# Order of the second sequence's norm, queries and folds in a fused two-layer kernel

## The reference, cut to what matters

```python
x = x + xattn0(layernorm(x), ctx, ctx, ..., key_mask)   # 8 heads of 4
x = x + ffn0(layernorm(x), ...)                         # below
x = x + xattn1(layernorm(x), ctx, mask, ...)            # 16 heads of 64
x = x + ffn1(layernorm(x), ...)                         # small inner nets

def ffn0(x):            # C = 128, 16 heads of 8, 4 experts
    h = conv3(layernorm(x, ln1_w, ln1_b))               # depthwise, causal
    q, k, v = split(h @ attn_w); q, k = rope(q), rope(k)
    p = softmax(causal(q @ k.T / sqrt(8)))
    x = x + (p @ v) @ proj_w
    h = layernorm(x, ln2_w, ln2_b)
    e = argmax(h @ router_w)
    return x + expert[e](h)
```

## Time and profile before

| | us |
|---|---|
| three runs | 340.04, 342.58, 346.72 (median 342.58) |
| profiled execution, its time | 340.81 |
| its span, first to last instruction | 338.6 |
| PE / DVE / ACT / POOL busy | 315.3 / 245.2 / 220.0 / 128.1 |
| mean granted clock of PE | 0.993 |

### The profile page before, as it was taken

The page is one execution under the profiler, slowest core; times in us unless marked ns, Lnnn a source line. Parts: engine busy times, 40 slices in busy tenths (PEclk is TensorE's granted clock), DMA queues, the critical chain, the costliest instruction groups (busy, mean ns, idle before and its releaser), DMA issues.

```text
span 338.6 us, 6802 instructions
## 1 busy us (share of the span) xinstructions
PE 315.3 (93%) x2270; PEld 220.6 (65%) x2270; DVE 245.2 (72%) x758; ACT 220.0 (65%) x649; POOL 128.1 (38%) x183
## 2 busy tenths in 40 slices
PE   8799989998989999999989998998999999999886
PEld 3348778665554433345446998985778687878675
DVE  4988875784898988888811552479788877887576
ACT  1488885375365756756676765754676667686995
POOL 3455564110641444410640440410685434535400
PEclk9999999999999999999998999999999999999999
DMA  7590000076763430091001003100100000000002
GB/s 213 196 274 10 2 0 2 8 243 170 209 206 89 113 102 3 1 326 52 5 31 56 2 31 111 33 1 2 54 20 15 0 2 1 3 0 0 2 0 65
DMA packets 21881, 22.47 MB, mean 66 GB/s; under 512 B 3894, under 2 KB 18646, under 8 KB 21846
## 3 DMA queue, kind: packets, MB, share of 16 engines
q1 hardware_dynamic: 18982, 16.78, 17.4%
q10 hardware_dynamic: 2352, 4.20, 3.7%
q0 software_dynamic: 512, 1.05, 1.0%
HBM read 14.22 MB, written 7.60 MB: 64 GB/s over the span
## 4 chain that ended last, share of the span: by engine, by line
PE 58%; DVE 16%; ACT 14%; issue 5%; POOL 4%; DMA 3%; SPq 0%; ACTq 0%; POOLq 0%
PE PS L1388 51%; PE PS L1442 5%; DVE PS L872 5%; ACT big L1167 5%; ACT big L1364 3%; POOL big L529 2%; DVE big L690 2%; DVE big L715 2%; DMA big<-in_A_WkT 2%; ACT big L1305 1%; ACT big L1141 1%; DMA XN<-scr_y,pos 1%; DVE XN L667 1%; ACT cw L1141 1%; PE PS L1704 1%
## 5 line engine op out<-in xcount | busy, mean ns | idle before, releaser
L1388 PE MATMUL PS<-big 128*128 128x128 f32 (+10 forms) x592 | 93.3, 308 | 7.0 <-DVE big L690 2.1
L1388 PEld LDWEIGHTS PS<-big 128*128 128x128 f32 (+3 forms) x592 | 56.2, 150 | 39.7 <-DVE mB L872 18.2
L529 POOL TENSOR_TENSOR big<-big,urec 128x1024 f32<-128x1024 f32 x24 | 45.6, 1900 | 60.2 <-DVE urec L722 45.4
L1167 ACT ACTIVATE big<-big 128x154 f32<-128x154 f32 x192 | 60.5, 319 | 10.6 <-DVE big L690 5.6
L872 DVE CUSTOM_DVE_ANT_0 PS<-PS,later 128x128 f32<-128x128 f32 (+3 forms) x128 | 60.1, 517 | 8.9 <-PE PS L1388 7.7
L1305 ACT ACTIVATE big<-PS 128x1024 f32<-128x1024 f32 (+3 forms) x64 | 43.2, 701 | 25.0 <-PE PS L1388 25.0
L1141 ACT ACTIVATE big<-PS 128x1280 f32<-128x1280 f32 (+2 forms) x30 | 32.3, 1088 | 27.0 <-PE PS L1442 24.5
L1388 PE MATMUL PS<-kkC,XT 128*128 128x462 f32 (+1 forms) x96 | 36.0, 511 | 1.9 <-DVE big L715 1.9
L1167 ACT ACTIVATION_READ_ACCUMULATOR big<-big 128x1 f32 x192 | 36.2, 189 | 0.0
L517 POOL TENSOR_TENSOR rstd<-ve,minus_half 128x4 f32<-128x4 f32 (+2 forms) x13 | 13.2, 1017 | 56.3 <-DVE ve L662 56.3
L1388 PEld LDWEIGHTS PS<-vwCm,big 128*128 128x128 f32 x256 | 30.8, 192 | 3.9 <-ACT big L1141 1.3
(11 more groups left out here) (192 smaller groups left out, 499.7 us busy)
## 6 DMA issues: line engine op xcount, KB each, us to landing
scr_qk<-big SPq DMA_DIRECT2D x12, 384.0 KB, 3.3
big<-scr_qk SPq DMA_DIRECT2D x16, 288.0 KB
big<-in_wv ACTq DMA_DIRECT2D x1, 2048.0 KB, 7.9
scr_x<-zrow SPq DMA_DIRECT2D x2, 448.0 KB, 6.9
scr_y<-big SPq DMA_DIRECT2D x2, 448.0 KB, 3.4
X<-in_x ACTq DMA_DIRECT2D x2, 256.0 KB, 3.3
big<-in_A_WoT ACTq DMA_DIRECT2D x1, 512.0 KB, 4.7
cw<-in_C_Wk SPq DMA_DIRECT2D x1, 512.0 KB, 5.2
```

The costliest lines, as they stand in the source:

```text
L529: pool.tensor_tensor(pn[:, 0:GH * P].rearrange("p (h k) -> p h k", h=GH), Pt[u % 3][:, :, 0:KM], r.to_broadcast([P, GH, KM]), ALU.mult).th ...
L1167: i = act.activation(Pt[u % 3][:, h, :], Pt[u % 3][:, h, :], ACT.Exp, accum_out=usum[:, u % 3, h:h + 1])
L1388: return pe.matmul(o, lhsT, rhs, start=start, stop=stop)
```

## The change

It moves work and adds none but one memset in place of ACT's copies.

- DVE: `ln_b_stats(1)` stands ahead of `add_rotated`, `ln_apply("b", U, XN, 1)` between it and `split_first`. `weigh_router` moves out of the ring's second step to behind `convolve(1)`.
- PE and ACT: the transpose of norm b and its copy come at fold 17 (were at 26), the second queries, keys and values ahead of fold 25 (were ahead of 30). Two banks take turns from fold 26 on (were from 32).
- PE: 28 folds stand ahead of m = 0 (were 32). Of the other 22 one stands behind each of the twenty steps, and a second behind steps 5 and 13 (`M_TWICE`).
- The waits of m = 0 are spread over m = 0, 1 and 2.
- POOL writes the ones and zeros of the first `vaug` with two memsets; ACT still copies the values, after the first copy of the maxima. For the second sequence ACT still writes all, ones with the zeros.

```diff
-        F_QKV = (14,30)
-        F_LN = 26
-        F_LATE = 32
-        F_VALUES = 42
-        F_MAX = 45
+        F_QKV = (14, 25)
+        F_LN = 17
+        F_LATE = 26
+        F_FIRST = 28
+        F_VALUES = 38
+        F_MAX = 41
+        M_TWICE = (5, 13)
...
             pool.wait_ge(part_ready[1], 3)
+            pool.wait_ge(preC_act, sum(j[2] for j in PREC[:F_VALUES]))
+            v = vaug[:, 0].rearrange("p t h m -> p (t h) m")
+            pool.memset(v[:, :, HDB:HDB + 1], 1.0).then_inc(v_ready, 1)
+            pool.memset(v[:, :, HDB + 1:32], 0.0).then_inc(v_ready, 1)
             split_maxima(1)
...
             ln_u_stats(1)
             rotate(0)
+            ln_b_stats(1)
             add_rotated()
+            ln_apply("b", U, XN, 1)
             split_first()
-            ln_b_stats(1)
-            ln_apply("b", U, XN, 1)
             convolve(1)
+            weigh_router()
             rotate(1)
...
-                if s == 1:
-                    weigh_router()
-                elif s == 3:
+                if s == 3:
                     centre_router()
...
                 copy(v[:, :, 0:HDB], XN[:, QT * b:QT * b + QT, :].rearrange("p t (h d) -> p (t h) d", h=HB)).then_inc(v_ready, 1)
-                copy(v[:, :, HDB:HDB + 1], ones[:, 0:QT * HB].unsqueeze(2)).then_inc(v_ready, 1)
 
             def no_values(b):
                 v = vaug[:, b].rearrange("p t h m -> p (t h) m")
+                copy(v[:, :, HDB:HDB + 1], ones[:, 0:QT * HB].unsqueeze(2)).then_inc(v_ready, 1)
...
-            copy_C(F_LN, F_VALUES)
+            copy_C(F_LN, F_MAX)
+            copy_maxima(0)
             act.wait_ge(preC_act, sum(j[2] for j in PREC[:F_VALUES]))
             values(0)
-            no_values(0)
-            copy_C(F_VALUES, F_MAX)
-            copy_maxima(0)
             copy_C(F_MAX, len(PREC))
...
                     if n == F_LATE:
                         pe.wait_ge(ln_T["b"], B)
-                        pe.wait_ge(qkv_read, 4 * B)
+                        pe.wait_ge(qkv_read, 4 * B - 2)
...
             queries_keys(1)
-            fold_C(F_QKV[1], F_LATE)
-            pe.wait_ge(preC_act, sum(j[2] for j in PREC[:F_LATE]))
-            pe.wait_ge(qkv_read, 4 * B)
+            fold_C(F_QKV[1], F_FIRST)
+            pe.wait_ge(preC_act, sum(j[2] for j in PREC[:F_LATE - 2]))
             pe.wait_ge(consts_ready, 2)
...
                     pe.wait_ge(s_max, m - 2)
+                elif m == 1:
+                    pe.wait_ge(qkv_read, 4 * B)
+                elif m == 2:
+                    pe.wait_ge(preC_act, sum(j[2] for j in PREC[:F_LATE]))
...
-            late = F_LATE
+            late = F_FIRST
             for m in range(M0):
                 scores_for_maximum(m)
-                if m >= 2 and late < len(PREC):
+                for _ in range(2 if m in M_TWICE else 1):
                     fold_C(late, late + 1)
                     late += 1
-                if late == F_MAX:
-                    turn_maxima(0)
+                    if late == F_MAX:
+                        turn_maxima(0)
```

More of the change, by code:

```diff
@@ L816, in ln_b_stats, with weigh_router @@
                 ln_stats("b", U, b, lambda: dve.wait_ge(ln_norm["u"], QT * b + QT))
+            def weigh_router():
+                dve.wait_ge(ld_b, 64)
+                dve.wait_ge(ld_vec, 16)
+                dve.wait_ge(zeroed, Z_ALL)
+                dve.tensor_scalar(rw2[:], rw[:], vec[:, V_LN2W:V_LN2W + 1], None, ALU.mult).then_inc(rw2_ready, 1)
+                dve.tensor_scalar(ln2b[:], ones[:], vec[:, V_LN2B:V_LN2B + 1], None, ALU.mult).then_inc(rw2_ready, 1)
             def convolve(b):
@@ L916, in x_plus_u @@
                 own.wait()
[L919 to L925, removed]
             def centre_router():
@@ L1662, in ring_scores @@
                 i.then_inc(s1_mm, 1)
-            late = F_LATE
+            late = F_FIRST
             for m in range(M0):
                 scores_for_maximum(m)
-                if m >= 2 and late < len(PREC):
+                for _ in range(2 if m in M_TWICE else 1):
                     fold_C(late, late + 1)
                     late += 1
-                if late == F_MAX:
-                    turn_maxima(0)
+                    if late == F_MAX:
+                        turn_maxima(0)
+            assert late == len(PREC)
             def outputs(s):
```

## The result

The changed kernel takes 347.49 us (median of 6 runs, 344.93 to 353.06) where the kernel before takes 341.57 (6 runs beside it, 339.29 to 349.91): a ratio of 1.0155 with a 95% interval of 1.0114 to 1.0195. Some executions of most kernels here run about 2% longer, at a mean clock of 0.975 or less (353.06 us at 0.961 is one); the medians hold them, the ratios and intervals leave them out. The change is slower, by less than 2%. The forecast was 341.8, in a range that ended at 344.8. The profiled execution took 347.92 us, with a span of 346.1 against 338.6.

What follows compares the result with a forecast made beforehand. TensorE, busy 93% of the span, was taken as the bound. Terms -0.5 (m = 0), +1.2 (steps), -0.3 (ring) gave +0.4: span 339.0, time 341.2, put at 341.8 given the median; forecast 340.3 to 343.4, with rivals 339 to 344.8.

Steps and rivals of the forecast that it cites:

- POOL's root is held up by the add: Second norm on POOL: the reciprocal root stands still until DVE's add is over, ending at 72.0; bounds no delay and 1.1 us.
- I had taken 21.4: Twenty steps from m = 0 to the ring: 21.4 us instead of 20.16, within bounds of 21.2 and 22.0.
- second form of rival 1: Lead on PE with a stack that is no limit at all: ring starts at 106.0, -2.0 us.
- mere stretching of the root: Alternative reading on POOL: the root is stretched by 0.38 us beside the add; the sum would be 0.7 us lower.
- rival 1: The lead before m = 0 arrives whole: -0.9 or -2.0 us, time 339.8 to 340.9; chance 0.2.
- Shifted by 4.7 the stack is there at 87.3: First stack before m = 0: the split starts 4.7 us later, PE waits 2.2 us, m = 0 starts 0.5 us sooner.
- rival 2: PE's clock falls after the wait at m = 0: up to 1.8 us lost, 343.6; chance 0.2 (long form 356, 0.03).
- 4.95 from the bytes moved: First stack's loads: issued at 77.65, home at 82.1 by the bytes moved, signalled at 82.6.
- my 0.5 for the signal: End of the first stack's loads: 0.5 us from bytes home at 82.1 to the signal at 82.6.
- my upper bound of 88: Start of m = 0: latest 88, if the first loads were home 0.7 later than the bytes say.
- the 0.3 us that I took off for the router: In the ring: router's operations no longer stand among the maxima, so PE's 0.30 wait goes; -0.3, bounds 0 and -0.6.
- forecast span of 339.0: Whole kernel: span goes from 338.6 to 339.0 by a sum of +0.4 us.

Runs made afterwards that it cites:

- hold: Changed kernel plus 18 unused matmuls on PE in the wait before m = 0: 344.74 us, ratio to before 1.0027; run again, 343.24 us, 1.0033.
- early stack: Changed kernel with sequence 0's first stack filled early from a tile of ones, its two loads left out: 340.12 us, ratio to before 0.9924.
- only DVE's order: Kernel before with VectorE's order alone changed, second norm ahead of the first sequence's split: 346.26 us, four runs, too few for a ratio.
- the folds put back: Changed kernel with its four early folds back ahead of m = 0, 32 there and none doubled: 340.25 us, ratio to before 0.9951.
- better version: Kernel before plus POOL's memsets, earlier router operations, spread m = 0 waits, and one fold moved ahead of the second queries: 338.85 us, ratio 0.9917.
- the small parts: Kernel before with only POOL's two memsets for ScalarE's copies and the router's operations behind the second convolution: 341.16 us, ratio 0.9955.

## Why the prediction was wrong

**What held.** POOL's root is held up by the add: it took 1.85 us and was over at 71.93 (forecast 72.0). The Trainium skill ("SBUF — State Buffer", Who interferes with whom) has this exclusion for a whole instruction, and this case's traces agree: 1.85 us beside the add, 1.01 without it, and an end 0.86 us behind the add's. The apply came at 71.96 (72.15), the split at 73.00 (73.25), the first write at 73.70 (74), the queries at 78.95 (79.2), and PE stood before m = 0 at 84.77 (85.1). The steps at whole clock are 21.43 us, as two kernels show, hold and, within 0.4, early stack (84.50 to 106.27 is 21.77); I had taken 21.4. The second form of rival 1 came out at -2.3 where I had -2.0. Two side sums were wrong: mere stretching of the root would have put the stack 0.5 us sooner, not 0.7 (71.5 against 72.0), and rival 1's times, -0.9 and -2.0 against the forecast's +0.4, come to 340.5 and 339.4, not 340.9 and 339.8.

**The step that failed** is "Shifted by 4.7 the stack is there at 87.3. This wait is the new one, 2.2 us long", and with it the chance and price of rival 2. The stack was there at 88.97, and the wait 4.21. Two terms of it were too small. The loads were issued at 83.45, not 82.35: from first write to first load it took 1.4 us longer than in the earlier trace rows, though the first write itself was 0.3 us sooner than forecast. And from that issue to m = 0 it was 5.52 us where I had 4.95 from the bytes moved; in the six traces where this wait shows it is 5.16 to 5.54. In the kernel before this term lay behind slack, so my 0.5 for the signal had no row; my upper bound of 88 covered this half and not the writes.

**What it set off.** I gave the fall of the clock a chance of 0.2 and a price of up to 1.8 us, worked out from a stretch of 3.6 us at half clock. With a wait of 4.2 us it came in most runs, lasted 6.8 us, and took 2.8 us from the steps. The Trainium skill ("TensorE: Matmul & The Clock Gate", Why this matters for your kernels) advises against idle gaps between bursts of matmuls; the hold, which has the same late stack without the gap, agrees, with 21.43 us against 24.19. The waits of 3.92, 3.93 and 4.10 us in three other traces had the half clock behind them, the 1.18 of the kernel with only DVE's order had not, nor had the waits of 0.33, 0.42 and 0.47 with the folds put back.

**In the ring** the 0.3 us that I took off for the router did not come. In the better version, which moved the router's operations too, the wait is still 0.30 us, and the ring's first step 110.79 - 105.81 = 4.98 us, as before. So the router's operations were not what PE waited for there.

**The sum,** for the profiled execution against the forecast span of 339.0: stack 1.7 (88.97 against 87.3), half clock in the steps 2.8, ring's first part 6.46 instead of 4.68, 1.8, and 0.8 behind that: 346.1. Of the ring's 1.8, 1.5 us is the second fall, at 115 to 119. It is not the change's own: the traces of the hold, of DVE's order alone and of the small parts have one there as well (a clock of 0.50 at 113 to 116 in the first), the better version's and that of the folds put back have none, and the one shown of before has none. But the kernel before has such falls too: its trace has one of 3.4 us at 177 to 181, and about half of its runs have mean clocks of 0.990 to 0.995, where one of 3.4 us takes 0.005. So the 1.5 us belong only in part to the difference.

The last 0.8 can be followed along the chain of waits, before and then after, at three places that answer to each other:

```profile
191.04 15.72 PE PS L1388 x141
...
225.20 0.44 PE PS L1403 x4
...
258.03 0.88 DVE stats L656 x4
```

```profile
197.65 11.76 PE PS L1391 x93
...
233.14 0.44 PE PS L1406 x4
...
265.48 0.88 DVE stats L662 x4
```

The changed kernel is 6.61 us behind at the first, 7.94 at the second and 7.45 at the third: 1.3 us are lost and 0.5 come back. The traces of the hold, of DVE's order alone and of the small parts lose 1.5 to 1.6 and win back 0.5 at the same places, so the moved folds are not the cause. The trace of before may simply be a short one here: its span of 338.6 us at a clock of 0.993 lies below the other runs of that kernel at 0.993, 339.1 to 341.0.

**Against the kernel before,** at whole clock, the change costs 1.7 us by the hold's runs (1.1 by the one undisturbed run of the changed kernel): m = 0 is 1.1 us later, the steps are 1.3 us longer for four folds, and 0.7 comes back behind the ring's start, of which the traces show the 0.5 above. The rest of the 3 to 5 us is clock.

**What stays open** is why the writes took longer. In the changed kernel all 16 DMA engines are busy until 81.5, and then 33 GB/s run until the loads are issued; from 81.75 to 83.25 it is 27 GB/s at a share of 0.07, about one engine of the 16 (331 GB/s over 16 is 21 each). In the kernel before they all end by 77.2. From first write to first load it is 8.35, 8.36 and 8.38 us in the three traces that write at 69.3 to 69.5, and 9.41 to 9.81 in all nine traces that write from 73.5 on. Queue 8, one of the two that load instructions, has a transfer of 16 KB there, some 0.94 us long; it lies within the writes in those nine traces and behind them, at 78.0 to 78.2, in the three others. Whether that is the cause was not tried. A transfer of 8 KB on the other such queue lies within the writes of those three, at 70.1 to 70.5. The Trainium skill ("DMA: Bandwidth & Descriptors", Why a DMA increments its semaphore by 16 and not by 1) says that a transfer counts as done only when the last of its engines has landed its part, so that one late engine holds the whole. The slow end at about one engine's rate, with the loads issued behind it, agrees; the trace doesn't name the engines.

## What to carry to other kernels

A step that moves on one engine moves its transfers too: before an earlier start of the bound engine is counted, ask what its next instruction waits for from a queue, and carry that whole chain (last write, signal, issue, load, signal) with the shift, not the bytes alone. If the bound engine would reach that wait early, leave it work to do there: four folds of 0.5 us put in front of the wait were worth 5.8 us, half of it by the clock. And when a new wait on TensorE comes out at some microseconds, price it with the half clock behind it, not by its length.

## What the runs showed that was not expected

- Idle time of 3.9 to 4.2 us on TensorE was followed by 6.8 us at 1.2 GHz in all four traces that have it, partly the wait itself and then dense work, 2.8 us lost; 18 products without a use in that time prevented it in both traces of the hold. By the mean clocks it didn't come in three of the 14 compared runs of the changed kernel.
- TensorE also falls to 1.2 GHz where only short waits stand before it: at the ring's start the last one was of 0.61 us, some 2 us earlier, then it was busy for 0.84 to 1.00 of each us, and the clock was at 0.50 for 3.4 us (115 to 119 in the changed kernel, 113 to 117 in the hold). This comes and goes between runs of one kernel; the kernel before has the same wait of 0.61 us and no fall there. Each 0.005 of mean clock went with about 1.5 us of span.
- Six writes of 384 KB, from the issue of the first to that of the load behind them, took 8.4 us in three traces and 9.4 to 9.8 us in nine.
- A load of 0.59 MB in two transfers, with more loads queued behind it, took 5.2 to 5.5 us from the issue of the first until the waiting engine started.
